# One bound per batch and head as the bias of the exponentials, instead of rows of bounds per query in the score products

## What is computed

```python
def ffn(x):      return quantised(x) @ quantised(w).T + bias
def attn(x):                                   # 16 heads of 8 features
    Q, K, V = heads(x @ Wq + bq), heads(x @ Wk + bk), heads(x @ Wv + bv)
    scores = einsum('bhqd,bhkd->bhqk', Q, K) / sqrt(8)
    mask = sigmoid(pattern(q, k, phase[h]) / temperature)     # same for all batches
    scores = scores + 0.3 * log(mask + 1e-6)
    return merge(softmax(scores) @ V) @ Wo + bo
x = x + 0.5 * ffn(layernorm(x))
x = x + attn(layernorm(x))
x = x + 0.5 * ffn(layernorm(x))
```

## Time and profile before

| | |
|---|---|
| median of three runs | 846.21 us (844.81 to 848.28) |
| profiled execution, device time | 850.78 us |
| its span in the profile | 848.9 us |
| mean granted TensorE clock | 0.959 |
| busy: PE, ACT, DVE, POOL | 736.3 (87%), 648.6 (76%), 540.4 (64%), 193.2 us (23%) |
| moved by DMA | 162.10 MB, mean 191 GB/s |

### The profile page before, as it was taken

One profiled execution on the slowest core, in us unless ns is written; L12 is line 12 of the kernel. 1 busy time (PEld: TensorE's weight loads), 2 busy tenths in 40 slices (PEclk: granted clock), 3 DMA queues, 4 the chain that ended last, 5 costly groups with the idle time before them and its releaser, 6 DMA issues.

```text
span 848.9 us, 12809 instructions
## 1 busy us (share of the span) xinstructions
PE 736.3 (87%) x4337; PEld 259.6 (31%) x4337; DVE 540.4 (64%) x1382; ACT 648.6 (76%) x773; POOL 193.2 (23%) x163
## 2 busy tenths in 40 slices
PE   0565738898999999989899999999999999999996
PEld 0143311322233323332323234223331232331175
DVE  8977877556989737997676446675342346532245
ACT  1568597787888887877788888888888888888841
POOL 0405672003443212263022021342030002000010
PEclk9986957999999999999999999999999999999998
DMA  5539558996767675765956746687758555556301
GB/s 148 113 123 350 204 148 317 326 243 200 222 206 231 205 202 176 189 207 120 272 159 206 227 126 208 194 227 228 204 193 226 188 166 172 176 175 208 96 1 55
DMA packets 56076, 162.10 MB, mean 191 GB/s; under 512 B 14130, under 2 KB 24506, under 8 KB 45586
## 3 DMA queue, kind: packets, MB, share of 16 engines
q1 hardware_dynamic: 51780, 154.37, 59.6%
q0 software_dynamic: 1776, 5.93, 2.1%
q10 hardware_dynamic: 2446, 0.89, 0.5%
HBM read 117.86 MB, written 43.29 MB: 190 GB/s over the span
## 4 chain that ended last, share of the span: by engine, by line
PE 48%; DVE 17%; ACT 15%; issue 9%; DMA 6%; SPq 3%; POOL 1%; DVEq 0%; ACTq 0%; POOLq 0%
PE S_PS L1756 18%; PE O_PS L1774 17%; ACT BIG L819 12%; DVE S_PS L1282 6%; DMA BIG<-shift_rows 6%; PE F_PS L1655 3%; SPq L430 2%; SPq L433 1%; PE R_PS L1784 1%; PE P_PS L1692 1%; DVE ST L1007 1%; PE F_PS L1645 1%; PE P_PS L1696 1%; ACT BIG L877 1%; PE P_PS L1645 1%
## 5 line engine op out<-in xcount | busy, mean ns | idle before, releaser
L819 ACT ACTIVATE BIG<-S_PS 128x1024 f32<-128x1024 f32 x512 | 505.2, 1023 | 116.8 <-PE S_PS L1756 113.7
L1756 PE MATMUL S_PS<-BIG 98*128 98x512 bf16 x1024 | 307.3, 390 | 43.0 <-DVE S_PS L1282 14.1
L1774 PE MATMUL O_PS<-BIG,VXP 128*18 128x512 f32 (+2 forms) x2048 | 271.7, 604 | 0.0
L1282 DVE COPY S_PS<-BIG 128x512 f32<-128x512 f32 x256 | 159.8, 687 | 175.6 <-ACT BIG L819 173.4
L1756 PEld LDWEIGHTS S_PS<-BIG 98*128 98x128 bf16 x1024 | 79.1, 98 | 299.8 <-ACT BIG L819 138.6
L645 POOL TENSOR_TENSOR XDT<-PART 128x512 bf16<-128x512 f32 x24 | 29.0, 1206 | 315.1 <-ACT PART L782 315.1
L1774 PEld LDWEIGHTS O_PS<-BIG,VXP 128*18 128x18 f32 (+2 forms) x2048 | 34.3, 95 | 101.5 <-issue 94.2
L620 POOL TENSOR_TENSOR X<-X,BFH 128x512 f32<-128x512 f32 x16 | 24.1, 1525 | 146.2 <-ACT BIG L853 113.1
L870 ACT ACTIVATE BIG<-S_PS,TEMP 128x1024 f32<-128x1024 f32 x32 | 34.3, 1111 | 20.7 <-PE S_PS L1947 20.4
L661 POOL TENSOR_TENSOR PART<-PART 128x512 bf16<-128x512 f32 x28 | 37.1, 1325 | 29.9 <-DVE PART L1190 29.9
L620 POOL TENSOR_TENSOR BIG<-BIG,BFH 128x512 f32<-128x512 f32 x16 | 20.9, 1332 | 98.5 <-DVE BIG L1107 84.4
(11 more groups left out here) (212 smaller groups left out, 758.6 us busy)
## 6 DMA issues: line engine op xcount, KB each, us to landing
BIG<-ln_masks SPq DMA_DIRECT2D x62, 1024.0 KB, 6.8
ln_masks<-BIG SPq DMA_DIRECT2D x16, 1024.0 KB, 6.2
BIG<-q_parts SPq DMA_DIRECT2D x63, 192.0 KB
BIG<-k_parts SPq DMA_DIRECT2D x63, 144.0 KB
BIG<-q_parts SPq DMA_DIRECT2D x63, 128.0 KB
q_parts<-PART SPq DMA_DIRECT2D x9, 768.0 KB, 3.8
k_parts<-PART SPq DMA_DIRECT2D x18, 384.0 KB, 4.5
BIG<-k_parts SPq DMA_DIRECT2D x63, 96.0 KB
```

The source lines that it names most:

```text
L819: act.activation(E[:, m % 2, j, 2 * pair:2 * pair + 2, :], S_PS[:, pair, :, :], ACT.Exp, scale=LOG_WEIGHT)\
L1282: ve.tensor_copy(S_PS[:, pair, i, :], LNM[:, slot, 2 * pair + i, :]).then_inc(s["seeded"], 1)
L1756: mm = pe.matmul(S_PS[:, pair, i, :], KT[0:ALL_ROWS, slot, K_COL[j], 128 * kb:128 * kb + 128], QT[0:ALL_ROWS, slot, j, :], start=False, st ...
L1774: mm = pe.matmul(O_PS[32 * j:32 * j + ahead + HD + 1, :], VXP[:, slot_of(n), at - ahead:at + HD + 1], E[:, m % 2, j, kb, :], start=kb == 0 ...
```

## The change

It makes one bound for each batch and head instead of one for each query: the root of (largest |q|² times largest |k|²). It stands in a tile `SHIFT` (128 partitions, one column per batch and head) and goes into each exponential as its bias, one value per partition. The score products keep 96 rows. Norms of q and k come from two products L1650 and L1651 into 32 rows of one bank; VectorE takes the largest (`top`), ScalarE its Ln (32x1), VectorE spreads it over two diagonals side by side (`top_diag`), one product of ones with them (`bound_product`) adds the two logarithms and gives the sum to all partitions, and ScalarE's Exp with scale 0.5 makes the root (128x16). All stores and loads of shift rows go, with their waits on TensorE and SyncE. The first exponential of a quarter waits for its bounds. In the prologue the order of TensorE's steps is changed, and a good part of the ticks is set anew. (In the diff L1715 is the matmul of `norms_k` before.)

```diff
-K_LOADS = 16 * (2 * len(GROUPS) + 1)
-FIRST_LOADS = 16 * 2 * len(GROUPS)
+K_LOADS = 16 * 2 * len(GROUPS)
...
-CHAINS = ((43, 59, 75, 91), (3, 27, 51, 83), (3, 27, 51, 91), ())
-CLOSE = dict(norm_ve=-2, turn_pe=3, xnt_act=3, q_pe=5, q_act=4, hi_q_ve=6, mid_q_ve=11, k_pe=9, k_act=9, hi_k_ve=10,
-             mid_k_ve=14, norms_k_pe=15, k_top_ve=17, norms_q_pe=19, sq_ve=19, sqrt_act=22, v_pe=13, v_ve=14,
-             row_ve=23, turn_bound_pe=25, bound_act=26)
+CHAINS = ((43, 58, 75, 91), (3, 27, 51, 83), (3, 27, 51, 91), ())
+CLOSE = dict(norm_ve=-2, turn_pe=3, xnt_act=3, q_pe=4, q_act=4, hi_q_ve=6, mid_q_ve=11, k_pe=9, k_act=9, hi_k_ve=10,
+             mid_k_ve=17, norms_pe=15, top_ve=17, top_act=19, diag_ve=19, v_pe=13, v_ve=14, bound_pe=21, bound_act=21,
+             row_ve=23)
...
-        def load_shift(engine, m):
-            ...
-            engine.dma_start(QT[QK_ROWS:ALL_ROWS, slot, :, :], SHIFT_D[n % 2, :, :, h, :])\
-                  .then_inc(s[stack_name(m)], 16)
...
-                    if i < NH - 1:
-                        load_shift(sp, m + 1)
...
-                    if i == (c + SECOND[q]["bound_act"]) // STEPS:
-                        store_shift(q + 1, j)
...
-            sp.wait_ge(s["bound_copied"], 1)
-            for t in range(T):
-                sp.dma_start(QT[QK_ROWS:ALL_ROWS, 0, :, 128 * t:128 * t + 128],
-                             CB4[T * head_of(0) + t:T * head_of(0) + t + 1, :, :, :]).then_inc(s["first_shift"], 16)
             load_stack(sp, 1)
...
+            def top_ln(n, j, size=1):
+                c = calls_of_bounds(n, j)
+                act.wait_ge(s["top"], 2 * (n * QB + j + size))
+                act.wait_ge(s["top_diag"], c)
+                act.activation(TOP[:, j:j + size], TOP[:, j:j + size], ACT.Ln).then_inc(s["top_ln"], 1)
+            def bound_exp(n, j, size=1):
+                c = calls_of_bounds(n, j)
+                act.wait_ge(s["bound_psum"], c + 1)
+                act.wait_ge(s["bound_row"], 3 * c)
+                act.activation(SHIFT[:, n % 2, j:j + size, :].rearrange("p j h -> p (j h)"), R_PS[:, 0:NH * size], ACT.Exp, scale=0.5)\
+                   .then_inc(s["bound_exp"], 1)
...
+                if k == 0 and m % NH == 0 and is_short(n):
+                    act.wait_ge(s["bound_row"], 3 * (1 + QB * n))
...
-                act.activation(E[:, m % 2, j, 2 * pair:2 * pair + 2, :], S_PS[:, pair, :, :], ACT.Exp, scale=LOG_WEIGHT)\
+                act.activation(E[:, m % 2, j, 2 * pair:2 * pair + 2, :], S_PS[:, pair, :, :], ACT.Exp, scale=LOG_WEIGHT,
+                               bias=SHIFT[:, n % 2, j, head_of(m):head_of(m) + 1] if is_short(n) else 0.0)\
...
+                bank = O_PS if n == 0 else R_PS
+                pe.matmul(bank[0:2 * NH, :], HSEL[:, NH:3 * NH], SQR[:, 1, :], start=True, stop=False)
+                pe.matmul(bank[0:2 * NH, :], HSEL[:, 0:2 * NH], SQR[:, 0, :], start=False, stop=True).then_inc(s["norms"], 1)
-            def norms_q(n, j):
-                at = 80 * j if n == 0 else 0
-                pe.wait_ge(s["k_top"], 2 * (n * QB + j) + 2)
-                for t in range(T):
-                    pe.matmul(R_PS[:, at + NH * t:at + NH * t + NH], SQR[:, 0, 128 * t:128 * t + 128], HSEL[:, :],
-                              start=True, stop=True)
-                pe.matmul(R_PS[:, at + 64:at + 64 + NH], ONES[:, :], KDIAG[:, :], start=True, stop=True)\
-                  .then_inc(s["norms_q"], 1)
-            def turn_bound(n, j, normed):
-                ...
+            def bound_product(n, j, normed, size=1):
+                c = n * QB + j - QB + 1 if past(n) else 0
+                pe.wait_ge(s["top_diag"], c + 1)
+                pe.wait_ge(s["bound_exp"], c)
+                if past(normed):
+                    pe.wait_ge(s["o_normed"], normed)
+                pe.matmul(R_PS[:, 0:NH * size], ONES[:, :], DIAG[:, j:j + size, :].rearrange("p j h -> p (j h)"),
+                          start=True, stop=True).then_inc(s["bound_psum"], 1)
...
-                    mm = pe.matmul(S_PS[:, pair, i, :], KT[0:ALL_ROWS, slot, K_COL[j], 128 * kb:128 * kb + 128],
-                                   QT[0:ALL_ROWS, slot, j, :], start=False, stop=True, skip_group_check=True)
+                    mm = pe.matmul(S_PS[:, pair, i, :], KT[0:QK_ROWS, slot, K_COL[j], 128 * kb:128 * kb + 128],
+                                   QT[0:QK_ROWS, slot, j, :], start=False, stop=True, skip_group_check=True)
```

290 lines of the change are left out of this document (103 added, 187 removed).

## The result

The changed kernel is slower. In the first measurement it took 858.73 us (median of 4, 854.16 to 864.31) against 847.25 for the kernel before, a ratio of 1.013 (95% interval 1.0082 to 1.0178). In a second, later one (a_again) it was 862.87 against 845.76, 1.0227 (1.018 to 1.0274). Forecast were 842.1 us and a range to 854. The profiled execution took 854.16 us, the shortest of its kernel's times; the one of before, 850.78, is near the top of that kernel's times (of 96 that were timed beside the experiments, one was longer, 851.36). So the two profiles are only 3.4 us apart, where the medians are 11.5 and 17.1 apart.

A forecast was written before the change was run, and what follows sets the result against it. Neither TensorE nor ScalarE was taken to bound alone; they pass work to and fro. 850.78 + 10 − 3.2 − 0.4 (logs) − 5.5 − 5 = 846.7 profiled, less 4.57: 842.1 us, range 832 to 854.

The forecast's parts named there:

- The bias, +10: Attention's exponentials: a per-partition bias adds 0.09 us each, about 100 of 512 on the chain of waits; +10 us.
- rival A: Attention's exponentials: the bias stays hidden in ScalarE's idle time, costing 4 instead of 10; 832.1 us, chance 0.14.
- The transfers, −5.5: Stacks before scores: 8 stops each one place of 0.68 us shorter, SyncE freed earlier; −5.5 us, bounds −1 and −10.
- The prologue, −3.2: Before attention: TensorE's stops for KDIAG ahead of `norms_q` go, sigmoids follow sooner; −3.2 us, bounds −1 and −5.5.
- The bounds in attention, −5: Twelve batches: KDIAG waits go (−5.9), less ScalarE work (−1.1), 2 given back; −5 us, bounds −7 and 0.
- The feared wait of ScalarE at the new Ln: Attention: ScalarE waits for VectorE's maxima, 2 us given back; over 1 us in more than three batches refutes the mechanism.
- The reference point: Whole kernel: terms taken against the profiled 850.78 us, then 4.57 subtracted to reach the median 846.21.
- rival B: Every head's boundary: ScalarE becomes the bound, about 0.36 us a head, 23 instead of 10; 855.1 us, chance 0.18.

The follow-up runs named there:

- the repaired one: Changed kernel with SyncE's waits restored at the twelve places and GpSimd's fill of the ones rows moved: 852.00 us, 1.0081 of before.
- b_memset: Kernel before with GpSimd's fill of the ones rows moved to after the first residue of batch 1: 843.35 us, 0.9954.
- b_noload: Kernel before without the loads of shift rows, 96 rows in the score products: 842.66 us, 0.9957.
- b_mem_masks: Kernel before with the fill of the ones rows moved and two mask stores issued earlier: 839.25 us, 0.9923.
- b_nowait: Kernel before without loads of shift rows, their stores in the attention and SyncE's waits for the bounds: 850.44 us, 1.0063.
- b_ptr: Kernel before with the exponentials' bias read from a column of zeros instead of the constant: 856.89 us, 1.0137.
- the repair tried: Changed kernel with SyncE waiting for the stack of head 0 to land before issuing that of head 1: 863.04 us, 1.0217 of before.
- a_imm: Changed kernel with the exponentials without their bias, bounds still computed but unused: 848.19 us, 1.0016 of before.
- b_order: Kernel before with only TensorE's prologue order changed, pattern products and projection of k ahead of `norms_q`: 848.01 us, 1.0022.
- the moved fill: Changed kernel with GpSimd's fill of the ones rows moved behind its chains: 854.85 us, 1.014 of before.

## Why the prediction was wrong

- **The bias, +10.** Right in kind and size: 10.7 in the old order, 10.3 in the repaired one, 14.7 (or 9.6 by the first measurement) in the order as changed. 1115 ns, 0.28 in head 62 and the risen share of the chain all came as described. Its idle time fell to 90.4 us and not to 75. The free bias (rival A) is refuted.
- **The transfers, −5.5: this is the step that failed.** The sum said that 8 stops become a place shorter, and that SyncE's freedom from ScalarE's copies "may help the later heads". The first half is true: 3.5 us without the loads, and the stops inside the attention went from 13.2 us to 5.6 and 9.8. The second has the wrong sign: the waits held each next mask back until the stack before it was further on its way, and without them 7.8 us are lost. The term, measured on the kernel before, is +4.3 instead of −5.5. The rows for it were in the trace of before: at the stack of head 39, L443, its last transfer, at 553.23, then L480, which waited until 555.44, then the mask, L490, at 556.11. I read the wait as a cost because SyncE was idle in it, and did not ask what it kept off the DMA engines. Nor did the sum have a term for the granted clock, which after some of these stops fell to 1.2 GHz; in the profiled pair that is 2.8 us.
- **The prologue, −3.2.** The product's wait did go and the sigmoids took 5.0 us less from their own start (80.39 to 105.67, against 76.69 to 106.98), near the bound I had set. But the stretch of before is not one number: the same instructions took 26.3 to 30.2 us in the traces of b_memset, b_noload, b_mem_masks, b_nowait and b_ptr, and 24.8 to 25.3 in all those of the changed order. What was missed is what is late next: the stack of head 0. I had noted that the first exponential follows the logs directly, and that SyncE would pass its wait some 4 us earlier, and did not ask what its transfers do to stack 0, issued by GpSimd in the same microseconds. It cost 3.2 us, and the repair tried only moved the loss into heads 1 to 7. So the start and quarter 0 are bound by transfers together. The first exponential came at 126.1 and 124.6, not near 121.
- **The bounds in attention, −5.** About right as a sum, wrong in its parts. In a_imm, which has no operand, the eight heads behind the old wait are 0.29 to 0.86 us shorter each, 3.1 together, not 5.9: the idle time before their seventh exponential went from 0.85 to 1.16 down to 0.14 to 0.50 and mostly not to 0.27, probably since the second product of 512 columns now stands there. The other heads from 8 to 45 in which no stack is late give 1.0 more, moved ticks included; 4.2 in all. The feared wait of ScalarE at the new Ln never came (at most 0.11 us).
- **The reference point.** All gains were read from an execution of 850.78 us, and 4.57 taken off at the end. Some of the stops counted as savings belonged to that execution alone. b_memset and b_order run the same attention, and their heads 22, 23, 25 and 26 are 4.9 and 5.6 us shorter together. In the profile of before the granted clock stood at 1.2 GHz from 382.6 to 386.0 and from 416.7 to 420.1 us, right behind stops for the stacks of heads 23 and 26; in those two it stayed at 2.4 GHz there.

The sum with the measured terms: 10.7 (bias) − 3.5 (loads) + 7.8 (waits) − 4.2 (bounds and ticks) = +10.8 against before, prologue at about 0; measured 11.5 and 17.1. Without the bias it is +0.1, and a_imm measured 1.0016. The slower side had been given to rival B, ScalarE as the bound at 0.36 a head and 23 us in all. Single heads of the last quarter show 0.18 to 0.52, 0.31 on average, and all 64 together 10 to 15 us, so B is not what happened, and no rival had SyncE's waits.

The wide spread of the changed kernel (854 to 869 us over both measurements) is in part explained: stops for stacks that differ from execution to execution, with or without a stretch at 1.2 GHz behind them. Open are what decides whether the clock falls at a stop (it did at one of 1.86 us in before and not at one of 2.27 in the changed kernel), and how much of the 8.0 us that the moved fill seemed to give the changed kernel is the fill's.

## What to carry to other kernels

Before removing a wait from a queue that issues transfers, list what stands behind it in that queue and what is in flight at that moment: an idle issuing engine can be what keeps a large transfer from sharing the DMA engines with an urgent smaller one. An operand read per partition on 512 instructions was priced here by the share of them on the chain of waits (100 of 512); 10 was forecast and 10.7 and 10.3 measured, with 14.7 in a third, noisier pair. A saving read from one profile is to be checked against a second execution, since stops, and TensorE's clock behind them, differed by 5 to 6 us between two executions of the same code. And if a gain is worked out at a start, name the next thing that is late there before it is counted.
